# A state-space stage worked in another order within each round, with one matmul per decay block in place of two

## The reference

```python
zxbcdt = hidden_states @ W_in                      # z 256, xBC 512, dt 4
xBC = silu(causal_dwconv(xBC, conv_w, conv_b))     # x 256, B 128, C 128
dt = softplus(dt + dt_bias);  A = -exp(A_log)
dA_cs = cumsum(dt * A)
diff = dA_cs[i] - dA_cs[j]
Lmat = where(j <= i, exp(diff), 0.0)
scores = einsum('bcihn,bcjhn->bcijh', C, B) * Lmat
y = scores applied to (x * dt), + state carried over + x * D
y = y * silu(z);  y = y * rsqrt(mean(y * y) + eps) * norm_w
return y @ W_out
```

## Time and profile before

| | |
|---|---|
| Median of 3 runs | 843.13 us (841.78 to 845.5) |
| The profiled execution | 851.88 us, of which span 849.8 us |
| Attention and first ffn | 0 to about 413 us |
| Start of the state-space part | about 413 to 465.8 us |
| Rounds 2 to 17 | 465.8 to 758.5 us |
| Second ffn | 758.5 to 849.8 us |
| Busy over the span | PE 755.9 us (89%), DVE 616.2 (73%), POOL 559.6 (66%), ACT 530.7 (62%) |

### The profile page before, as it was taken

The page is one execution under the profiler, slowest core; times in us unless marked ns, Lnnn a source line. Parts: engine busy times, 40 slices in busy tenths (PEclk is TensorE's granted clock), DMA queues, the critical chain, the costliest instruction groups (busy, mean ns, idle before and its releaser), DMA issues. The chain is left out here.

```text
span 849.8 us, 15933 instructions
## 1 busy us (share of the span) xinstructions
PE 755.9 (89%) x5114; PEld 553.2 (65%) x5114; DVE 616.2 (73%) x1725; ACT 530.7 (62%) x1023; POOL 559.6 (66%) x923
## 2 busy tenths in 40 slices
PE   3589999999999887999888899899979999869997
PEld 2478888888888774666644566566646556546665
DVE  3568878877887536888668787887888676638885
ACT  3234344444434244888548788788868788728886
POOL 1567667766776404787723797589758866848775
PEclk9979999999999897999759899999999999979999
DMA  4341221111111020000200000000000000000112
GB/s 124 89 126 43 60 69 30 29 43 43 30 29 45 16 83 29 0 1 0 76 1 9 1 1 10 0 1 9 3 0 2 9 1 2 1 1 26 50 50 76
DMA packets 59996, 25.83 MB, mean 30 GB/s; under 512 B 22288, under 2 KB 59152, under 8 KB 59664
## 3 DMA queue, kind: packets, MB, share of 16 engines
q1 hardware_dynamic: 59920, 24.90, 11.0%
HBM read 15.26 MB, written 9.63 MB: 29 GB/s over the span
## 5 line engine op out<-in xcount | busy, mean ns | idle before, releaser
L1444 DVE SCALAR_TENSOR_TENSOR arena<-bank,convw_sb,arena 128x510 f32<-128x510 f32 (+2 forms) x192 | 142.4, 744 | 31.7 <-ACT arena L954 27.0
L719 POOL TENSOR_TENSOR arena<-arena 128x768 f32<-128x768 f32 x64 | 114.8, 1814 | 12.6 <-ACT arena L981 12.4
L701 POOL TENSOR_TENSOR arena<-ff,arena 128x512 f16<-128x512 f32 x64 | 73.5, 1158 | 24.8 <-ACT arena L923 22.7
L1824 PE MATMUL bank<-xnT,win_sb 128*128 128x512 f32 x128 | 73.7, 660 | 2.9 <-DVE arena L1444 2.9
L918 ACT ACTIVATE ff<-bank 128x512 f32<-128x512 f32 x96 | 56.3, 586 | 29.5 <-PE bank L1747 29.3
L632 POOL TENSOR_TENSOR leafV<-leafV,leaf_tmp 32x14 f32<-32x14 f32 (+6 forms) x224 | 62.2, 277 | 17.5
L822 ACT ACTIVATE ff<-bank 128x256 f32<-128x256 f32 (+2 forms) x80 | 33.9, 424 | 57.4 <-PE bank L1568 36.3
L1276 DVE SCALAR_TENSOR_TENSOR ff<-bank,ff 128x512 f32<-128x512 f32 x96 | 64.7, 683 | 6.1 <-ACT ff L918 3.4
L725 POOL TENSOR_TENSOR arena<-arena 128x512 f32<-128x512 f32 x32 | 40.3, 1268 | 40.9 <-DVE arena L1451 40.5
L1855 PE MATMUL bank<-arena 128*64 128x256 f32 (+1 forms) x512 | 49.8, 338 | 19.4 <-DVE x_all L1333 18.5
L628 POOL TENSOR_TENSOR leaf_tmp<-leafV 32x14 f32<-32x14 f32 (+6 forms) x224 | 56.3, 251 | 16.4
(11 more groups left out here) (194 smaller groups left out, 2173.1 us busy)
## 6 DMA issues: line engine op xcount, KB each, us to landing
LT_dram<-arena SPq DMA_DIRECT2D x16, 256.0 KB, 2.3
ff<-R_dram SPq DMA_DIRECT2D x16, 256.0 KB, 2.8
out<-x_all SPq DMA_DIRECT2D x8, 512.0 KB, 3.2
x_all<-in_L_attn_a_x SPq DMA_DIRECT2D x7, 512.0 KB, 5.6
slabs<-in_tables SPq DMA_DIRECT2D x2, 1024.0 KB, 6.1
ff<-in_tables SPq DMA_DIRECT2D x2, 768.0 KB, 4.3
x_all<-in_L_attn_a_x SPq DMA_DIRECT2D x2, 256.0 KB, 3.8
R_dram<-tab SPq DMA_DIRECT2D x2, 256.0 KB, 6.8
```

The source lines that it names most:

```text
L701: nc.gpsimd.tensor_tensor(of_block(hl[u], j), hidT[u][:, j, :], of_block(hh[u], j), ALU.subtract).then_inc(hl_done[u], 1)
L719: nc.gpsimd.tensor_tensor(score[h], cb[g % 2], hgam[h], ALU.mult).then_inc(score_done, 1)
L1444: nc.vector.scalar_tensor_tensor(acc_of[:, :, s:SEQ], src_of[:, :, 0:SEQ - s], convw_sb[:, r, TAPS - 1 - s:TAPS - s], acc_of[:, :, s:SEQ], ...
L1824: mm(conv_bank[r % 2][:, :], win_sb[:, INNER + r * P:INNER + (r + 1) * P], xnT[b % XNT_SETS][:, :], start=True, stop=True).then_inc(conv_m ...
```

## The change

Two things change, both in the state-space part.

**One matmul per decay block.** The second matmul of `log_decay` is gone. The slabs get 63 constant rows more, which put -30000 on pairs of positions (2k, 2k+1) that come later, so that everything above the diagonal is masked but the element inside a pair. Its exponent stays finite, because each step is now held at -88 and above (before at -128). The remaining element is removed on the other factor: `causal_products` on POOL zeroes `cb` above the diagonal, two `affine_select` of 128 x 2 x 128 per round, and `score_of` waits for them. Three copies on DVE that prepared the constants during the first ffn are gone.

**Another order within a round** on PE, ACT, DVE and POOL. The waits between engines are those of before.

```diff
-FLOOR = -128.0
+FLOOR = -88.0
...
+            def causal_products(g):
+
+                pool.wait_ge(cb_done, done(turned_pair(g, 0)))
+                for batch in range(BATCHES):
+                    diagonal = cb[g % 2][:, batch * TRI:(batch + 1) * TRI].rearrange("p (s c) -> p s c", c=P)[:, 0:3:2, :]
+                    last = nc.gpsimd.affine_select(out=diagonal, in_=diagonal, compare_op=ALU.is_ge, fill=0.0, base=0,
+                                                   pattern=[[0, 2], [1, P]], channel_multiplier=-1)
+                last.then_inc(causal_done, 1)
+
             def score_of(g, h):
 
                 pool.wait_ge(hgam_done, done(decay_at(g, h, 0)))
-                pool.wait_ge(cb_done, done(turned_pair(g, 0)))
+                pool.wait_ge(causal_done, done(g))
...
@@ POOL
                 if f is not None:
                     gated_y(f, 1)
+                if x is not None:
+                    ln_rstd_of(*x)
+                if f is not None:
                     pool.wait_ge(ysq_done, done(INNER_BLOCKS * f + 1))
                     nc.gpsimd.tensor_tensor(ysq[0][f % 2], ysq[0][f % 2], ysq[1][f % 2], ALU.add).then_inc(ysum_done, 1)
-                if x is not None:
-                    ln_rstd_of(*x)
-                if e is not None:
+                if e is not None:
+                    causal_products(e)
                     score_of(e, 0)
-                    score_of(e, 1)
...
                 if e is not None:
+                    score_of(e, 1)
                     score_of(e, 2)
                     score_of(e, 3)
+                    gated_y(e, 0)
                 if diff_q is not None:
                     diffs(diff_q)
                 if split_q is not None:
                     split_sums(split_q)
-                if e is not None:
-                    gated_y(e, 0)
...
@@ PE
                 mm(to[:, 0:TRI], from_slab[side][j][:, at * P:(at + 1) * P], to_rows[side][:, at * TRI:(at + 1) * TRI],
-                   start=True, stop=False)
-                mm(to[:, 0:TRI].rearrange("p (s c) -> p s c", c=P)[:, 0:3:2, :], ident16[:, :],
-                   never16[:, :].rearrange("p (s c) -> p s c", c=P), start=False, stop=True).then_inc(E_mm, 1)
+                   start=True, stop=True).then_inc(E_mm, 1)
...
```

## The result

The changed kernel is slower: 854.25 us median (848.15 to 857.81) against 847.54 for the kernel before in the same runs, a ratio of 1.0076 (95% interval 1.005 to 1.0102). The forecast was 834.5 us, 1% faster than the 843.13 it started from. The profiled execution took 853.4 us, its span 851.6.

What follows compares the result with a forecast made beforehand. DVE's loop through four engines was taken to decide, PE 1 to 2 us behind. Round-group terms (-3.5, -0.9, -0.3, 0, -4.6, +0.7) sum to -8.6 us, taking the median from 843.13 to 834.5 us; range 820 to 850.

Steps and rivals of the forecast that it cites:

- Rounds with `split_sums` just before (4, 8, 12): Splits now stand between the two gated_y and delay the second; rounds taken at 18.1 us, round 8 having taken 18.61.
- the order gives nothing: Rival, chance 0.13: removing the matmul opens gaps on PE, its clock falls, gains of rounds 13 to 15 are lost; 843 us.
- Rounds 5 and 9 are DVE's ... 20.3 after 20.70: With the softplus ahead of the residual, only the 1.26 us wait ahead of skip shrinks, by 0.4 us.
- Starved scans: Rival, chance 0.20: DVE's second scan waits for three POOL scores, 5.4 us a round in rounds 3, 7, 11; 849 us.
- Rounds 1 and 2 ... -3.5: Round 2, 20.58 us before, should come to its kind's 18.1 or a little less; round 1 gains half a microsecond.
- Rounds 16 and 17: Tail of 28.28 us, where only scores are awaited, so the zeroing is not covered: 0.7 us longer.
- What is added: Two affine_select on POOL between cb's arrival and the first score, 0.75 us a round, covered where POOL idles for skip.
- the zeroing costs much more: Rival, chance 0.05: the strided in-place zeroing takes much more than 0.75 us, slower from 2 us a round on; 850 us.
- What is removed ... 0.88 us a round: Eight second matmuls a round on PE at 0.11 us each; at most 14 us in 16 groups, only where PE is the bound.
- rounds 13 to 15: Undisturbed rounds, PE-bound: 16.79 us less 0.88 of matmuls less 0.65 idle gives 15.26 each, -4.6 us for three.
- Rounds 3, 7 and 11: Diffs delay the second gated_y, plus 1.3 us of scans and a 1.0 us stall: 21.0 us, 20.0 without layer norm.
- POOL's move costs nothing: Rival, chance 0.22: the second gated_y is off the path, six rounds fall by 2 us each; about -21, 822 us.

Runs made afterwards that it cites:

- e4: Changed kernel plus 32 small idle matmuls on PE behind conv(b,2) in rounds 3, 4, 7, 8, 11, 12 (and 15): 846.18 us, ratio 1.0006 to before.
- e7: Kernel before with only the zeroing on POOL added, two matmuls and old order kept: ratio 1.0079 to before.
- e8: Changed kernel with the second matmul of each decay block back, zeroing and new order kept: ratio 1.0078 to before.
- e14: Changed kernel with POOL's diffs and split_sums back ahead of the first gated_y, and softplus_middle with half the series behind the residual: 839.52 us, ratio 0.9898 to before.
- e1: Changed kernel with two matmuls per decay block and no zeroing, so the new order alone: ratio 1.0035 to before.
- e3: Changed kernel with POOL's diffs and split_sums back in their old place ahead of the first gated_y: 845.82 us, ratio 0.9972 to before.
- e2: Kernel before with one matmul per decay block and the zeroing on POOL, old order kept: ratio 1.0075 to before.
- e11: Changed kernel plus 36 small idle matmuls on PE ahead of the first head_outputs of rounds 16 and 17: 853.8 us, ratio 1.0074 to before.

## Why the prediction was wrong, by its own steps

- **The step that failed** is the pricing of delays at PE's full clock. "Rounds with `split_sums` just before (4, 8, 12)" put every matmul behind the wait at its full-clock duration ("then 0.9, W_out 1.78, gate and the next conv 0.86 each") and came to 18.1. The chain up to there was right within 0.1 us (second `gated_y` 9.58 for 9.6). Without the fall the rounds are 18.46 (e4), with it 20.14 and 20.99. Rounds 3, 4, 7 and 8 together took 82.36 us; the forecast was 78.2 and e4's 77.06. The third rival, "the order gives nothing", named the fall and got 0.13. It put it down to the matmul taken away, which e7 and e8 contradict, and priced it at 0.7 us for one group of matmuls, where round 8 shows 2.5. Between -8.6 and +7.1 us lie 15.7, of which rounds 3, 4, 7 and 8 are 4.2; my estimate from the traces is that 5.3 us of the clock lie in these rounds (82.36 - 77.06), 1.3 in the tail (below) and, if e14's trace is typical, 3.4 in round 1, some 10 in all.
- **"Rounds 5 and 9 are DVE's ... 20.3 after 20.70"** was wrong by 1.2 each: the three scores in a row, which the change makes by moving the power, stall three of the softplus's operations (0.80, 1.18 and 1.73 us for 0.18, 1.15 and 0.22). I searched for this stall at the scans only. There it hardly came: in rounds 3 and 7 they ran in 0.67 and 0.65 us, in round 11 in 1.16, beside the end of a score, and 0.65. The power, for whose length I had counted 1.0 us, didn't hold them. DVE and POOL in round 7:

```profile
580.56 0.67 DVE L1425 TENSOR_TENSOR_SCAN ff<-ones_col,ff 32x256 f32<-32x256 f32 x1
581.16 0.65 DVE L1426 TENSOR_TENSOR_SCAN ff<-ones_col,ff 32x256 f32<-32x256 f32 x1
```

```profile
580.72 1.32 POOL L788 TENSOR_TENSOR arena<-arena,half_neg 128x4 f32<-128x4 f32 x1 [0.33 <-DVE arena L1497]
```

*Starved scans* fell as a place and held as a mechanism.
- **"Rounds 1 and 2 ... -3.5"** was +2.35 (52.94 to 55.29): up to the cut at `taps(1,3)` round 1 grew by 3.4 us (32.36 to 35.72), and round 2 lost 1.0 (20.58 to 19.57) for the 2.5 forecast. I priced round 2 by its kind and gave round 1 half a microsecond, and never followed the lists in round 1, which lost their special places for conv(1,1) and the first taps. Putting these back takes 3.5 us off (55.40 to 51.93), and e14's one trace says that they are the clock's again.
- **Rounds 16 and 17, "+0.7"**, were +3.6. The order alone gives +0.6 (e1, 28.91). The zeroing alone costs +0.46 in the old order (e7, 28.74) and 1.2 in the new one (e8 30.08); the rest, 1.8, came with one matmul, of which the clock is 1.3: e3 has the same lists there and took 30.61 at a PEclk of 0.79 in round 17, after 31.92 at 0.56. What the remaining half microsecond is stays open.
- **"What is added" had the zeroing right** (0.76 us for two, forecast 0.75) **and its cost wrong**: it was taken as covered outside the tail. e7 shows +6.75 us in the part, in rounds 4 and 8 1.98 us each for 0.76 by way of the shift, and e1 against e8 0.4% in the new order, with intervals that overlap. So the fourth rival, "the zeroing costs much more", was right in that it costs more than it takes, but not by its reason, as the strided form itself took 0.40 us.
- **"What is removed ... 0.88 us a round"** as the most it can give, and only where PE is the bound: it gave 0 in the old order's rounds 13 to 15 (16.80 in e2) and 0.28 in the new one's (15.21 for 15.49), as PE then waits 0.76 us for POOL's last score:

```profile
701.65 1.52 PE L1863 MATMUL bank<-arena 128*64 128x256 f32 x16 [0.76 <-POOL arena L731]
```

- **Right in number, in part by luck**: rounds 13 to 15 came to 15.2 (forecast 15.26), but of the 1.58 the matmul gave 0.28 for 0.88 and the order 1.31 for 0.65, two errors that cancel. Rounds 3, 7 and 11 came to 20.97, 20.26 and 19.82 (forecast 21.0, 21.0, 20.0), but the stall of 1.0 us in that sum didn't come, and the clock at 0.92 in round 3 and 0.91 in round 11 filled its place; e4 has 20.25 and 19.88 in rounds 3 and 7 at full clock. 11 and 12 took 37.20 for 37.32 (forecast 0), 6 and 10 took 18.51 and 18.10 (forecast 18.1). *POOL's move costs nothing* fell: e3 takes 8 us off by undoing it.

Sum, forecast and measured: rounds 1 and 2 -3.5 and +2.35; 3 to 6 -0.9 and +2.8; 7 to 10 -0.3 and +3.1; 11 and 12 0 and -0.1; 13 to 15 -4.6 and -4.7; 16 and 17 +0.7 and +3.6; together -8.6 and +7.1.

## What to carry to other kernels

A wait that opens a hole on PE costs the hole and can cost the matmuls behind it at half clock; where the trace has PE at 2.4 GHz with holes of a microsecond, price each added hole with both durations, and see whether an order closes it before filling it with idle work. When a busy GpSimd instruction is moved, or several are joined, look at the small DVE operations that will now stand beside it: those with two inputs in on-chip memory, and `tensor_scalar`, are late by what is left of that instruction; the reciprocal was not (0.55 us beside a score and without), nor anything beside the power. And a list written by hand has special places for its first rounds (and, as e4's round 15 shows, a condition on the round number can take in one more round than was meant); follow them one by one when the list is made uniform.

## What the runs showed of the hardware

- In these rows the stall of DVE beside GpSimd is all or nothing and ends with the GpSimd instruction that was running when it began. Of two-input operations the shift took 0.73, 1.24 and 1.62 us in three orders, ending each time within 0.1 us of POOL's instruction. It also caught a `tensor_scalar` with a single input in on-chip memory, 0.80 and 0.88 us for the 0.20 of its like at 625.58. The taps, which read one input from PSUM, took 2.30 us for three beside a score and without one. The Trainium skill, in SBUF — State Buffer, "Who interferes with whom", says that a DVE instruction with two SBUF inputs contends with a GpSimd instruction that reads SBUF, and that `tensor_scalar` can contend too; the rows agree.
- The power on POOL is an exception, though it reads on-chip memory: in round 7 the second scan, with two inputs, began 0.44 us after it and ran free in 0.65 us. The power itself took 1.32 us beside the scans, for the 1.02 of its like in round 8.
- The clock of the same stretch of the same work is not the same from one kernel to the next: round 12 at 0.83 in e11 and 1.00 in the changed kernel, and round 8 at 1.00 and 0.84, with equal lists; a hole of 1.97 us in round 1 that left the clock up, and one of 2.02 that did not, rounds 3 and 7 of the changed kernel at 0.92 and 1.00. The changed kernel's runs follow it loosely: the shortest, 848.15 us, had a mean granted clock of 0.948, the longest, 857.38 and 857.81, had 0.930 and 0.938, but one of 851.3 had 0.935.
